# A decoder block on one core: score banks swapped at the seam of the two attentions, group 1 turned earlier, a semaphore for each tile's keys, twice as many up banks

## The reference, cut to what matters

```python
# 1. self attention, 8 heads, per row of 64 tokens
dots = einsum('bhid,bhjd->bhij', q, k) * SCALE        # q, k = split(x @ W_qk)
attn = softmax(dots + bias)                            # bias from conv[:, clipped distance]
x = layernorm(x + (attn @ v) @ W_out + b_out)
# 2. gated cross attention, 4 heads (q from x, k and v from the context)
log_D = cumsum-difference of log_sigmoid(fg) + ig      # lower triangle, ig, fg = [q,k,v] @ w
D = exp(log_D - max_log_D)
C = (q k^T / sqrt(dh)) * D
h = C / (max(|sum C|, exp(-max_log_D)) + eps) @ v      # then a norm per head, * (1 + ln_weight)
x = layernorm(x + h)
# 3. one shared expert, and the best 2 of 8 routed experts (gelu, 128 -> 512 -> 128)
x = layernorm(shared(x) + sum_k gate_k * expert_k(x) + x)
```

## Time and profile before

| | us |
|---|---|
| runs: median (lowest, highest), 3 runs | 464.09 (463.42 to 466.31) |
| the profiled execution's own time | 463.78 |
| its span (first to last instruction on the core) | 462.0 |
| PE, DVE, ACT, POOL busy | 437.0, 304.1, 303.3, 184.3 |
| mean granted TensorE clock | 0.985 of full |

### The profile page before, as it was taken

The page is one execution under the profiler, slowest core; times in us unless marked ns, Lnnn a source line. Parts: engine busy times, 40 slices in busy tenths (PEclk is TensorE's granted clock), DMA queues, the critical chain, the costliest instruction groups (busy, mean ns, idle before and its releaser), DMA issues.

```text
span 462.0 us, 14470 instructions
## 1 busy us (share of the span) xinstructions
PE 437.0 (95%) x5114; PEld 371.2 (80%) x5115; DVE 304.1 (66%) x965; ACT 303.3 (66%) x675; POOL 184.3 (40%) x209
## 2 busy tenths in 40 slices
PE   8999999999988999999978999999999999999993
PEld 7688888888877777677645999989998999999631
DVE  5578888888888457887867677644444444555155
ACT  4678677876766799998748974456665664233236
POOL 5621122024501011115655765637777666554300
PEclk9999999999999899999979999999999999999998
DMA  4352322900000007102212143302333332311287
GB/s 140 86 145 54 94 67 78 257 23 4 2 26 25 2 27 250 50 26 71 65 34 74 47 111 88 87 25 73 86 88 86 92 86 82 82 53 36 67 294 215
DMA packets 47710, 38.11 MB, mean 82 GB/s; under 512 B 5168, under 2 KB 41008, under 8 KB 47648
## 3 DMA queue, kind: packets, MB, share of 16 engines
q1 hardware_dynamic: 42896, 28.16, 22.2%
q0 software_dynamic: 4320, 8.92, 5.8%
q10 hardware_dynamic: 432, 0.20, 0.1%
HBM read 19.30 MB, written 16.34 MB: 77 GB/s over the span
## 4 chain that ended last, share of the span: by engine, by line
PE 54%; DVE 17%; ACT 11%; issue 8%; DMA 6%; POOL 3%; SPq 1%; DVEq 1%; ACTq 0%; POOLq 0%
PE bank L1347 6%; PE bank L1433 6%; PE bank L1391 4%; PE bank L1401 4%; POOL routed L605 2%; DVE negmax L1565 2%; DVE prob L1562 2%; PE bank L1068 2%; PE bank L1015 2%; PE bank L1017 2%; PE bank L1016 2%; PE bank L1058 2%; PE bank L1420 2%; DVE tkr L1556 2%; PE bank L1421 2%
## 5 line engine op out<-in xcount | busy, mean ns | idle before, releaser
L605 POOL DMA_INDIRECT routed<-rh,zbuf x71 | 72.2, 1017 | 44.3 <-DVE rh L1940 28.8
L1940 DVE TENSOR_SCALAR rh<-bank,zbuf 128x128 f32<-128x128 f32 x71 | 24.8, 350 | 39.8 <-PE bank L1433 21.5
L1433 PE MATMUL bank<-wdn,prob 128*128 x400 | 49.5, 276 | 0.6 <-DVE rh L1940 0.4
L1433 PEld LDWEIGHTS bank<-wdn,prob 128*128 128x128 f32 x400 | 47.0, 192 | 1.4 <-DVE rh L1940 1.1
L502 POOL DMA_INDIRECT slots<-zbuf,slot x32 | 32.7, 1021 | 22.0 <-PE bank L1347 5.4
L940 ACT ACTIVATE prob<-bank 128x512 f32<-128x512 f32 x50 | 29.8, 597 | 13.7 <-PE bank L1422 10.8
L502 POOL DMA_INDIRECT slots<-tkr,slot x32 | 31.1, 972 | 13.8 <-issue 5.7
L492 POOL TENSOR_TENSOR hlw<-hst,lnw 128x512 f32<-128x512 f32 x8 | 10.3, 1284 | 59.1 <-ACT hst L815 59.1
L925 ACT ACTIVATE prob<-bank 128x512 f32<-128x512 f32 x21 | 12.5, 597 | 29.2 <-PE bank L1391 29.2
L1420 PE MATMUL bank<-xT_hi,wq_hi 128*128 128x256 f32 x100 | 30.3, 303 | 0.9 <-DVE xT_lo L1950 0.9
L1347 PEld LDWEIGHTS bank<-sdn,qblk 128*128 128x128 f32 x256 | 29.6, 192 | 0.5
(11 more groups left out here) (303 smaller groups left out, 1199.4 us busy)
## 6 DMA issues: line engine op xcount, KB each, us to landing
slots<-x2T SPq DMA_DIRECT2D x8, 585.0 KB, 5.2
zbuf<-slots SPq DMA_DIRECT2D x25, 130.0 KB
tkr<-in_x SPq DMA_DIRECT2D x8, 256.0 KB, 3.0
cs<-in_ctx SPq DMA_DIRECT2D x8, 256.0 KB, 2.9
wup<-in_L_ffn_routed_up SPq DMA_DIRECT2D x1, 2048.0 KB, 9.9
zbuf<-tkr SPq DMA_DIRECT2D x8, 256.0 KB
wup<-routed SPq DMA_DIRECT2D x8, 256.0 KB, 3.6
wdn<-routed SPq DMA_DIRECT2D x8, 256.0 KB, 4.3
```

The source lines that it names most:

```text
L605: pool.indirect_dma_start(routed, bass.IndirectOffsetOnAxis(ap=xr[n][:, :].bitcast(I32)[:, DEST:DEST + 1], axis=0), yr[n % 4][:, :], None) ...
L1433: m = mm(bank[6 + a][:, 0:D], hTp[:, q, c // 2, c % 2, a, :], wdn[:, bass.ds(e * (FC * D) + c * D, D)], start=(c == 0), stop=(c == FC - 1))
```

## The change

In words:
- `qk` writes to bank 4 for even tiles and bank 3 for odd ones (before: 3 and 4). The last shared chunk moves from bank 3 to 4, the shared down product of even groups from bank 4 to 3.
- PE's seam: `turn_x(1)` comes right after `turn_ctx(1)`, ahead of `heads(7, 3)`; 2 + 3 fillers go; in group 0 of stage B the order is `floors`, `out_turn(7, 3)`, `qk(0, 0)`, `proj(7, 3)`, `gates(1)`, the wait for all residuals, `qk(0, 1)`.
- ACT's seam: `turned_ctx(1)` and `turned_x(1)` come ahead of `maxima(0)`; then `floors(0)`, `oT_evac(7, 3)`, `decays(0, 0)`, `rsqrt_a(7)`, `decays(0, 1)`.
- DVE's seam: `head_out(7, 3)` comes ahead of `first_keys`.
- `al_ok` becomes four semaphores. `qk(g, k)` waits for the one of tile k (for group 0, for key copy k + 1). `front_rows(g)` waits for all four of group g - 1.
- Pair p's up product goes to banks 2 and 3 (even p) or 4 and 5 (odd p), and waits for the GELUs of pair p - 2.
- Some semaphores are merged, with their counts adapted (`stored`, `prep_ps`, `lnv_ok`).

The diff, cut:

```diff
+    al_ok = [sem(f"al_ok{k}") for k in range(GT)]
-    SH_BANK = [0, 1, 7, 3]
+    SH_BANK = [0, 1, 7, 4]
-    KEYS = 16 * GT
+    def d_bank(k):
+        return bank[4 - k % 2]
+
+    def down_bank(g):
+        return bank[(3, 5)[g % 2]]
+
+    def up_bank(q, b):
+        return bank[2 + 2 * q + b]
...
                 r = slice(k * HR, k * HR + NH)
-                sp.dma_start(al[g % 2][r, k, :, :].rearrange("p a s -> p (a s)"), arow[r, :]).then_inc(s["al_ok"], 16)
+                sp.dma_start(al[g % 2][r, k, :, :].rearrange("p a s -> p (a s)"), arow[r, :]).then_inc(al_ok[k], 16)
...
         oT_evac(NG - 1, 2)
+        turned_ctx(1)
+        turned_x(1)
         maxima(0)
-        oT_evac(NG - 1, 3)
-        rsqrt_a(NG - 1)
-        turned_ctx(1)
...
             if now:
                 floors(g)
+            if g == 0:
+                oT_evac(NG - 1, 3)
+                decays(0, 0)
+                rsqrt_a(NG - 1)
             if before:
                 heads_keep(g - 1)
             if g >= 4 and g % 2 == 0:
                 probabilities((g - 4) // 2)
-            if now:
+            if now and g > 0:
                 decays(g, 0)
...
         act.wait_ge(s["st_out"], 16 * (FILL_TILES // DUMP))
-        turned_x(1)
         group_b(0)
...
-                act.activation(prob[:, 2 * q + b, :], bank[2 + b][:, :], ACT.Gelu).then_inc(s["hT_ok"], 1)
+                act.activation(prob[:, 2 * q + b, :], up_bank(q, b)[:, :], ACT.Gelu).then_inc(s["hT_ok"], 1)
...
         turn_ctx(1)
-        filler(4, 2)
+        turn_x(1)
         heads(NG - 1, 3)
         proj(NG - 1, 2)
-        out_turn(NG - 1, 3)
-        turn_x(1)
-        proj(NG - 1, 3)
-        filler(4, 3)
...
                 pe.wait_ge(s["qblk_ok"], NH * g + NH)
-                if g == 0:
-                    pe.wait_ge(s["keys_ok"], GT)
-                else:
-                    pe.wait_ge(s["al_ok"], KEYS * g)
                 pe.wait_ge(s["rh_ok"], NH * (g + 1))
-            bk = bank[3 + k % 2]
+            if g == 0:
+                pe.wait_ge(s["keys_ok"], k + 1)
+            else:
+                pe.wait_ge(al_ok[k], 16 * g)
+            bk = d_bank(k)
...
             if now:
                 floors(g)
+            if g == 0:
+                out_turn(NG - 1, 3)
+                qk(0, 0)
+                proj(NG - 1, 3)
+                gates(1)
+                pe.wait_ge(s["res_ok"], NT + GT)
+                qk(0, 1)
+            elif now:
                 qk(g, 0)
                 qk(g, 1)
-            if after:
+            if after and g > 0:
                 gates(g + 1)
...
-        pe.wait_ge(s["res_ok"], NT + GT)
         for g in range(NG):
             group_b(g)
...
-                if c % 2 == 0 and not (isinstance(p, int) and p == 0):
-                    pe.wait_ge(s["hT_ok"], 2 * p - 1 + b)
-                u = bank[2 + b][:, (c % 2) * 2 * P:(c % 2 + 1) * 2 * P]
+                if c % 2 == 0 and not (isinstance(p, int) and p < 2):
+                    pe.wait_ge(s["hT_ok"], 2 * p - 3 + b)
+                u = up_bank(q, b)[:, (c % 2) * 2 * P:(c % 2 + 1) * 2 * P]
...
             if g > 1:
-                dve.wait_ge(s["al_ok"], KEYS * (g - 1))
+                for k in range(GT):
+                    dve.wait_ge(al_ok[k], 16 * (g - 1))
...
                 front_rows(0)
                 front_max(0)
-                first_keys()
...
         head_out(NG - 1, 3, ast)
+        first_keys()
         residual(NG - 1, 2)
         residual(NG - 1, 3)
         x1_out(NG - 1)
```

More of the change, by code:

```diff
@@ L237, in decoder_layer @@
     y0, y1, fin = (a[:, :].rearrange("p (t d) -> p t d", d=D) for a in (wup, wdn, x2T))
[L240 to L241 removed]
+    names = """ld_tok ld_tok1 ld_wqk ld_conv ld_hank bias_ok qzero_ok ld_attn ld_small ld_gw ld_wup ld_wdn ld_sh cpad_ok
+    const_p const_v wq_ok read_ok prep_ps gw_ok vsteps xT_ps xT_ok xhi_ok xlo_ok
     wqlo_ok z_ps z_ok s_ps v_ps v_ok logit_ok exp_ok pT_ps pT_ok av_ps o_ok oT_ps oT_ok pr_ps
     res_ok stat_ok mv_ok lnv_ok rstd_ok x1_ok asteps cs_ok x1T_ps x1T_ok cT_ps cT_ok g_ps
[L244 to L245 removed]
+    vc_ps nrm_ok nsq_ok fabs_ok fexp_ok flog_ok igsteps rh_ok mrow_ok emx_ok floor_ok qblk_ok
+    vals_ok dd_ps decay_ok c_ok u_ps h_ok hsq_ok hva_ok hn_ok hln_ok hrs_ok res1_ok mv1_ok
     rstd1_ok x2_ok bsteps x2T_ps lg_ps lg_ok lmax_ok lexp_ok tokb_ok lnd_ok fl_ps hlw_ok
[L247 removed]
+    tk_ok x2e_ok shift_ok rsteps hotb_ok rank_ps cum_ok slot_ok cnt_ok toff_ok iota_ok
     pre_ok mask_ok shu_ps sh_ok shd_ps shk_ps base_ok xr_ps xrT_ok up_ps wst_ok hT_ok y_ps y_ok passed_pool
[L249 removed]
+    passed_dve keys_ok passed_pe mv2_ok rstd2_ok fina_ok find_ok tot_ps stored st_out""".split()
     s = {n: sem(n) for n in names}
@@ L383, in _ @@
             row = sp.value_load(padi[0:1, e:e + 1], min_val=0, max_val=E * REG - P)
-            sp.dma_start(slots[bass.ds(row, P), :], slots[E * REG + e * P:E * REG + e * P + P, :]).then_inc(s["st_pad"], 16)
+            sp.dma_start(slots[bass.ds(row, P), :], slots[E * REG + e * P:E * REG + e * P + P, :]).then_inc(s["stored"], 16)
         sp.wait_ge(s["toff_ok"], 2)
@@ L408, in _ @@
             sp.wait_ge(s["find_ok"], D_TILES[g][1])
-            sp.dma_start(out_tok[:, r, :], fin[:, r, :]).then_inc(s["st_fin"], 16)
-        sp.wait_ge(s["st_fin"], 16 * NG)
+            sp.dma_start(out_tok[:, r, :], fin[:, r, :]).then_inc(s["stored"], 16)
+        sp.wait_ge(s["stored"], 16 * (1 + E + NG))
     @block.gpsimd
@@ L646, in oT_evac, with rsqrt @@
             act.activation(oT[:, :], bank[2 + k % 2][:, 136:136 + P], ACT.Copy).then_inc(s["oT_ok"], 1)
-        def rsqrt(mv_sem, need, src, ln_out, ln_sem, r_out, r_sem, count):
+        def rsqrt(mv_sem, need, src, ln_out, r_out, r_sem, count):
             act.wait_ge(mv_sem, need)
-            act.activation(ln_out, src, ACT.Ln, bias=eps[:, 0:1]).then_inc(ln_sem, 1)
-            act.wait_ge(ln_sem, count)
+            act.activation(ln_out, src, ACT.Ln, bias=eps[:, 0:1]).then_inc(s["lnv_ok"], 1)
+            act.wait_ge(s["lnv_ok"], count)
             act.activation(r_out, ln_out, ACT.Exp, scale=-0.5).then_inc(r_sem, 1)
@@ L804, in decays @@
             act.wait_ge(s["dd_ps"], GT * g + k + 1)
-            act.activation(decay[:, k % 2, :], bank[3 + k % 2][:, 256:512], ACT.Exp).then_inc(s["decay_ok"], 1)
+            act.activation(decay[:, k % 2, :], d_bank(k)[:, 256:512], ACT.Exp).then_inc(s["decay_ok"], 1)
         def heads_of(j):
@@ L1188, in _ @@
                 pe.wait_ge(s["ld_hank"], 16)
-                mm(bank[2][:, :], flip[:, :], hankel.rearrange("p h s -> p (h s)"), start=True, stop=True).then_inc(s["hank_ps"], 1)
+                mm(bank[2][:, :], flip[:, :], hankel.rearrange("p h s -> p (h s)"), start=True, stop=True).then_inc(s["prep_ps"], 1)
         pe.wait_ge(s["const_v"], 1)
@@ L1346, in sh_down_mm @@
                 for c in range(FC):
-                    m = mm(bank[4 + g % 2][:, k * D:(k + 1) * D], shT[g % 2][:, c, k * P:(k + 1) * P], sdn[:, c, :],
+                    m = mm(down_bank(g)[:, k * D:(k + 1) * D], shT[g % 2][:, c, k * P:(k + 1) * P], sdn[:, c, :],
                            start=(c == 0), stop=(c == FC - 1))
@@ L1665, in score @@
                 dve.wait_ge(s["u_ps"], t - 1)
-            stt(cmat[:, k % 2, :], bank[3 + k % 2][:, 0:256], DH ** -0.5, decay[:, k % 2, :],
+            stt(cmat[:, k % 2, :], d_bank(k)[:, 0:256], DH ** -0.5, decay[:, k % 2, :],
                 ALU.mult, ALU.mult).then_inc(s["c_ok"], 1)
@@ L1821, in base @@
             r = slice(g * GT, g * GT + GT)
-            stt(total_in[:, r, :], tok[:, r, :], 2.0, bank[4 + g % 2][:, :].rearrange("p (k d) -> p k d", k=GT),
+            stt(total_in[:, r, :], tok[:, r, :], 2.0, down_bank(g)[:, :].rearrange("p (k d) -> p k d", k=GT),
                 ALU.mult, ALU.add).then_inc(s["base_ok"], 1)
```

20 lines of the change are left out of this document (10 added, 10 removed).

## The result

| | before | after |
|---|---|---|
| runs side by side: median (lowest, highest), 21 each | 463.42 (461.19 to 466.31) | 461.39 (458.40 to 463.60) |
| profiled execution, its span | 463.78, 462.0 | 461.44, 459.7 |
| mean granted clock of it | 0.985 | 0.982 |

The ratio is 0.9951 (95% interval 0.9933 to 0.9969): 2.0 us faster, where 5.2 were forecast. 461.39 lies inside the stated 457.0 to 462.6 and outside the forecast's own 457.2 to 459.9. One percent was not reached. All ratios leave out executions more than 1.5% above the fastest of the same kernel: four of twelve in e13, one of twelve in e1 and in e9, none or one elsewhere.

A forecast was written before the change was run, and what follows sets the result against it. TensorE, busy 95% of the span, was taken as the bound, so only its holes, slow stretches and waits could give time. 2.3 + 0.15 + 2.8 = 5.25 us gave a median of 458.8 us; own range 457.2 to 459.9, stated 457.0 to 462.6.

The forecast's parts named there:

- The seam, 2.3 us: Between first and second attention: earlier first scores bring decays(0,1) to 153.2 from 155.53, a gain of 2.3 us.
- The shift of 2.3 passes through these groups whole: Groups 1 to 6: the seam's 2.3 us carries through undiminished, since all engines start from it.
- The last group, 2.8: Last attention group: scores start on the first key DMA, decays(7,0) and decays(7,2) come earlier, a gain of 2.8 us.
- the upper bound of 3.0: Last group: the largest gain allowed for its term, 3.0 us.
- The low bound of 0.7: Last group: the smallest gain allowed for its term, 0.7 us, with low clock until 239.8.
- The sum: Whole kernel: seam 2.3, groups 1 to 6 0.15 and last group 2.8 give 5.25 us.
- Up banks, 0 to 0.3: Expert pairs: twice as many up banks relax a wait with 1.1 us of slack; taken as 0, range 0 to 0.3 us.
- Added waits, 0: 24 more waits on TensorE and 18 on VectorE: taken as 0 us for those satisfied long before.
- seam stays low: Rival: the seam stays at the low clock and gains only 0.6 us, total 460.5 us; chance 18%.
- doesn't do what it says: Rival: ScalarE becomes late and the seam gives nothing, the last group only 1.3 us, total 462.6 us; chance 8%.
- last group keeps its low clock: Rival: low clock stays in the last group or VectorE holds more, gain there 0.7 us, total 460.9 us; chance 14%.
- its case of a clock that falls there and a gain of 0.6: Seam: the clock falls at 151.1 as before, decays(0,1) comes at 154.9, a gain of 0.6 us.

The follow-up runs named there:

- e13: The changed kernel with the fillers of e9 plus two more behind the router in group 4; median 461.73 us, ratio to before 0.9934.
- e1: The changed kernel with one key semaphore and the old two up banks, so the seam alone; median 462.58 us, ratio to before 0.9992.
- e9: The changed kernel with 14 filler matmuls in TensorE's waits or light work in groups 6 and 7; median 461.69 us, ratio to before 0.9972.
- e14: Unchanged copy of the kernel before, one profiled execution; second stage 155.30 us, mrow(0) to mrow(1) 10.49 us.
- e3: The kernel before with only the new up banks (four instead of two); median 463.64 us, ratio to before 1.0003.
- e2: The kernel before with only a key semaphore per tile, waited for tile by tile; median 461.75 us, ratio to before 0.9968.
- e12: The kernel before with 28 filler matmuls in groups 4 to 6 and ahead of the last group's scores; median 463.11 us, ratio to before 1.0002.
- e15: Another unchanged copy of the kernel before, one profiled execution; second stage 155.35 us, mrow(0) to mrow(1) 12.00 us.
- e7: The changed kernel with the old two up banks, so seam and per-tile keys; median 462.13 us, ratio to before 0.9971.
- e10: The changed kernel with twelve filler matmuls, each in a wait of TensorE; median 461.73 us, ratio to before 0.9982.
- e6: Unchanged copy of the changed kernel; median 461.13 us, ratio to before 0.9940.
- e11: The changed kernel with each wait for a tile's keys written twice, on TensorE and VectorE; median 461.32 us, ratio to before 0.9960.
- e16: Unchanged copy of e7, one profiled execution; second stage 152.67 us.
- e8: The kernel before with eight more fillers on TensorE ahead of out_turn(7,3) at the seam; median 464.63 us, ratio to before 1.0017.
- e5: Unchanged copy of the kernel before; median 463.30 us, ratio to before 0.9995.

## Why the prediction was wrong

- **The seam, 2.3 us: right as an interval, wrong as a gain.** All ten profiles of kernels with the new seam have 9.81 to 9.83 us from `mrow(0)` to `mrow(1)`, 2.2 less than the profile of before. The failed step is "The shift of 2.3 passes through these groups whole". The shift was still whole at `mrow(4)` (31.56 us behind `mrow(1)`, before 31.72) and had shrunk by 1.0 at `mrow(7)`. The step also assumed that the low clock belongs to the seam. And it took ScalarE alone for full in these groups (10.63 of 11 us), where the same row has TensorE at 10.31. Of the 2.2, 1.5 are a low stretch that three of seven profiles have there; when the clock is up (e14, e3, e2, e12) the old seam takes 10.5 and the new order saves 0.7.
- **The last group, 2.8: the mis-sized term.** It measured 1.6 (16.01 to 14.41 up to `decays(7,3)`), of which 1.3 at `decays(7,0)`, as forecast (0.4 against e3, e14 and e15, which have 5.7 us there). The other part assumed full clock in the last scores or a low one ending near 236; it lasted from 231.5 to 238.4. Where low clock does not fall there (e7, e9, e10) the same piece takes 12.2 us, a gain of 3.8, above the upper bound of 3.0. The low bound of 0.7 was meant for a low clock until 239.8 and was too low, since the scores do start 2.5 us after `mrow(7)`.
- **What was missing: a stretch in group 5, and VectorE behind GpSimd.** From `mrow(4)` to `mrow(7)` after takes 39.65 for 38.66: 0.2 more up to `mrow(5)`, 0.55 more up to `mrow(6)`, where the low stretch lies, and 0.2 more up to `mrow(7)`, with a VectorE instruction held in both. e6 and e1, without the stretch and with the instruction held for 0.3 us only, take 37.99 and 37.69. Of the 1.65 between after and e6, 0.5 lie in the piece with the stretch and 1.1 in the one with the longer hold. No term and no rival had low clock at a place where before shows none, nor a VectorE that waits for GpSimd.
- **The sum.** 2.2 + 0.2 (mrow 1 to 4) - 1.0 + 1.6 + 0.0 is 3.0 in the first pair of profiles; on average over the profiles without fillers the second stage went from 155.4 (before, its copies and e3) to 152.6 (after, e6, e7, e11 and e16), by 2.8. The rest of the program takes 158.0 to 160.8 us in whatever kernel. Single indirect DMAs of GpSimd there take 1.4 instead of 0.96 us, at other places in each profile, and the last reload takes 3.4 to 6.3 us; what each is worth was not separated. Before's own profile had one of the shortest, 158.2. The medians, 2.0 and 2.6 us apart (463.42 to 461.39, 463.77 to 461.13), agree with that within this jitter.
- **Up banks, 0 to 0.3: a little low.** 0.3 to 0.4 us at the first pairs in every profile, and 1.0 us between the medians of e7 and e6, whose intervals overlap. In e3, alone, the median did not fall. The slack of 1.1 us was read in the steady pairs; the first two have none.
- **Added waits, 0: right**, as far as e11 shows. The rivals "seam stays low" and "doesn't do what it says" did not occur; "last group keeps its low clock" did, at 460.9, and 461.4 was measured.
- The new order, with fewer fillers and as many turns, kept full clock at the seam in all its ten profiles. The Trainium skill (TensorE: Matmul & The Clock Gate, Part 4) says that a transpose doesn't count as busy for the clock gate as a matmul does, from which the prediction took its case of a clock that falls there and a gain of 0.6. These traces do not bear that case out, and they do not separate turns from holes either.

What stays open: that low clock moves rather than vanishes is shown for single pieces (e14, e16), and e8, with the seam held, has one stretch fewer than e14; why, and how the sum is set, isn't. The share of executions with a low seam rests on seven profiles.

## What to carry over

A slow stretch of TensorE in one profile is a draw, not a property of the place: take a second and a third profile of the kernel before, and compare a whole stage, before you book its removal as a gain. Then look at the other engines in the pieces that changed: here, of the 1.65 us between two executions of after in groups 4 to 6, 1.1 lie where TensorE ran at full clock and one VectorE instruction lasted until GpSimd had finished. What an order of instructions gives is the interval that repeats with the clock at the same level on both sides (here 0.7 us at the seam, to 0.02 us, and 0.4 to 1.3 at the last keys, where before itself varies by 0.9), and that is the part to forecast. If an edit takes waits out of TensorE, its slow stretches may cost more afterwards, as there is less idle time to hide them; the runs hint at this and do not show it.

## What the runs showed of the hardware

- Between 30 and 450 us the stretches at 1.2 GHz have two lengths, 3.41 and 6.83 us; their sum in a profile was 3.4, 6.8, 10.2, 13.7 or 17.1 us, in eighteen profiles of thirteen programs.
- Identical programs place them differently, and where there is none, the times repeat: `mrow(1)` to `mrow(4)` took 31.50 to 31.72 us in all eighteen.
- A VectorE instruction that overlaps GpSimd's `hlw` can last until that ends: it took 1.5 to 2.1 us for 0.2 to 0.3, ending 0.1 us behind `hlw`, in fourteen profiles, and 0.56 in the other four.
- Whether low clock costs more in the tighter kernel is open. Over 33 executions of after (two batches) the time falls by 230 us per 1.0 of mean clock (95 to 328), over 82 of before (batches of e1 and e5) by 133 (11 to 256); the intervals overlap. The seven of after at 0.987 or more have a median of 459.2, next to the forecast of 458.8; the 24 such of before have 463.3.
